# Row maxima subtracted by extra rows of the queries, fetched by DMA, in place of one-hot matmuls

## The reference

```python
# layer 0:  LN; softmax(q k^T * 9**-0.5) over keys; MLP = mixture of 4 experts, top 2
# layer 1:  LN; the same attention; one tanh-GELU MLP
# layer 2:  RMS norm; q and k of each head are RMS-normalised first:
def rmsnorm(x, g, d):
    n = jnp.linalg.norm(x, axis=-1, keepdims=True)
    return x / jnp.maximum(n, EPS) * d ** 0.5 * g        # g is qg for q, kg for k
# layer 3:  LN; attention over the 16 heads of one token, not over tokens
```

## Time and profile before

| | |
|---|---|
| runs, us | 1548.19, 1546.15, 1554.1 (median 1548.19) |
| profiled execution, us | 1548.05 |
| its span, us | 1546.1 |
| mean granted TensorE clock | 0.964 |
| PE busy | 1410.9 us, 91% |
| DVE busy | 1036.5 us, 67% |
| ACT busy | 779.5 us, 50% |
| POOL busy | 541.6 us, 35% |
| attention of layer 0 (first to last exponential) | 64.8 to 242.5 |
| of layer 1 | 585.4 to 756.0 |
| of layer 2 | 892.9 to 1097.8 |
| of layer 3 | 1224.7 to 1448.8 |

### The profile page before, as it was taken

The page is one execution under the profiler, slowest core; times in us unless marked ns, Lnnn a source line. Parts: engine busy times, 40 slices in busy tenths (PEclk is TensorE's granted clock), DMA queues, the critical chain, the costliest instruction groups (busy, mean ns, idle before and its releaser), DMA issues. The chain is left out here.

```text
span 1546.1 us, 41104 instructions
## 1 busy us (share of the span) xinstructions
PE 1410.9 (91%) x16016; PEld 1055.9 (68%) x16016; DVE 1036.5 (67%) x2601; ACT 779.5 (50%) x1287; POOL 541.6 (35%) x739
## 2 busy tenths in 40 slices
PE   5799988999999998999999688877999799998998
PEld 2377676777777776777777566666776577776776
DVE  4698885666776677888447689897355466665342
ACT  2377664333323336676555366665544365555543
POOL 3355542211131304554323324433335134343222
PEclk9799999999999999999999899999999799999999
DMA  4765631111122123554001333453207576774011
GB/s 129 161 151 155 148 95 52 51 44 44 36 70 70 33 73 87 144 146 120 20 29 46 105 94 92 110 129 86 45 24 108 90 109 114 132 131 93 25 54 47
DMA packets 209129, 134.94 MB, mean 87 GB/s; under 512 B 142461, under 2 KB 191320, under 8 KB 202730
## 3 DMA queue, kind: packets, MB, share of 16 engines
q1 hardware_dynamic: 188978, 129.74, 35.3%
q10 hardware_dynamic: 19960, 2.57, 1.2%
HBM read 98.24 MB, written 33.24 MB: 85 GB/s over the span
## 5 line engine op out<-in xcount | busy, mean ns | idle before, releaser
L1546 DVE TENSOR_REDUCE negm<-banks 128x8 bf16<-128x1024 f32 x256 | 311.0, 1215 | 81.4 <-PE banks L650 79.6
L1235 ACT ACTIVATE prob<-banks 128x1024 f32<-128x1024 f32 x256 | 262.5, 1025 | 191.9 <-PE banks L672 191.1
L1363 ACT ACTIVATE hid<-banks 128x512 f32<-128x512 f32 x144 | 86.0, 597 | 220.3 <-PE banks L961 220.2
L1977 POOL TENSOR_TENSOR X<-X,gx 128x288 f32<-128x288 f32 x128 | 104.1, 826 | 255.0 <-DVE gx L1576 253.2
L977 PEld LDWEIGHTS banks<-wfc,hid 128*128 128x128 f32 x1152 | 156.6, 190 | 29.9 <-issue 20.3
L668 PE MATMUL banks<-qk 54*128 54x128 bf16 (+1 forms) x2048 | 168.7, 236 | 5.3 <-ACT prob L1235 5.0
L672 PE MATMUL banks<-mT,identb 64*128 64x128 bf16 x2048 | 165.7, 225 | 0.9 <-issue 0.9
L977 PE MATMUL banks<-wfc,hid 128*128 128x144 f32 x1152 | 161.1, 286 | 0.0
L650 PE MATMUL banks<-qk 54*128 54x128 bf16 (+1 forms) x2048 | 122.9, 241 | 39.6 <-DVE negm L1546 24.9
L960 PE MATMUL banks<-hT,wfc 128*128 128x512 f32 x288 | 149.6, 601 | 2.4 <-DMA wfc<-in_L_cond_w 2.4
L684 PE MATMUL banks<-prob,V 128*32 128x128 f32 x4096 | 143.5, 282 | 0.0
(11 more groups left out here) (169 smaller groups left out, 2777.0 us busy)
## 6 DMA issues: line engine op xcount, KB each, us to landing
qk<-qk_scr SPq DMA_DIRECT2D x96, 216.0 KB
gbuf<-gate_scr SPq DMA_DIRECT2D x64, 288.0 KB, 4.5
qk_scr<-parts SPq DMA_DIRECT2D x48, 288.0 KB, 2.8
qk<-qk_scr SPq DMA_DIRECT2D x96, 144.0 KB
qk<-cw_scr SPq DMA_DIRECT2D x8, 1024.0 KB, 4.9
qk_scr<-parts SPq DMA_DIRECT2D x48, 144.0 KB, 2.4
qk<-qk_scr SPq DMA_DIRECT2D x96, 72.0 KB
qk<-tok_scr SPq DMA_DIRECT2D x32, 216.0 KB
```

The costliest lines, as they stand in the source:

```text
L1235: act.activation(prob[:, 2 * (U % 3):2 * (U % 3) + 2, :], pairs[1][:], ACT.Exp, scale=scale).then_inc(a_exp, 1)
L1546: dve.tensor_reduce(negm[:, u // 2, :, 4 * (u % 2):4 * (u % 2) + 4], pairs[0][:].rearrange("q s (h k) -> q s h k", k=T), AX.X, ALU.max, ne ...
L1977: pool.tensor_tensor(x, x, gx[:, q, :, :], ALU.add).then_inc(g_x, 1)
```

## The change

In layers 0 to 2 an operand of `scores` has 62 rows instead of 54. On the side of the keys the 8 new rows of each half are constants: row j is one for head j and zero for the others; SyncE loads them from `io.picks`, once for each slot, and slot 1 again before group 10, since layer 0's MLP uses that room. On the side of the queries row j holds row j of `mT`, repeated for all 8 heads; ScalarE issues two DMAs for each pair, from `mT` into `qk`, right behind the exponential of an even unit, three units ahead of the one that needs it (`row_of_maxima`); the first two pairs of a layer go ahead of its first exponential. `scores` waits for these DMAs (q_m) instead of for `mT`. The one-hot matmuls stay in layer 3 alone.

In layer 2 `head_norms` is gone from VectorE. GpSimd's `scale_heads` multiplies the factors by the gain (two operations), then q and then k by the factors, all four sequences in one operation each. It stands ahead of `parts23` of the same group, behind `copy_rest` of the group before, and in layer 1's MLP behind `factor`. VectorE does Newton rounds 2 and 3 both at unit 0.

```diff
+RM = KS
-        def operand(l, side, n, U, s, i):
+        def operand(l, side, n, U, s, i, more=0):
-            rows = KS if l < 3 else KS + TB
+            rows = KS + more if l < 3 else KS + TB
...
+            def picking_rows(r):
+                for s in range(2):
+                    row = 64 * s + RM
+                    sp.dma_start(qk[row:row + 8, 1, r].rearrange("j h t -> j (h t)").bitcast(F32), io.picks).then_inc(q_one[r], 16)
...
-                    pe.wait_ge(d_qn, CR + 8 * (n - 16) + (8 if m else 4))
+                    pe.wait_ge(g_qn, CR + 2 * (n - 16) + (2 if m else 1))
...
-                pe.wait_ge(d_mt, CR + U // 2 + 1)
+                if l < 3:
+                    if u == 0 and n in (0, 1, 2, 10):
+                        pe.wait_ge(q_one[n % 3], 64 if n == 10 else 32)
+                    if u % 2 == 0:
+                        pe.wait_ge(q_m[U // 2 % 2], 32 * (U // 4 + 1))
+                else:
+                    pe.wait_ge(d_mt, CR + U // 2 + 1)
                 for i in range(4):
                     at = slice(T * i, T * i + T)
                     for s in range(2):
-                        pe.matmul(bank[2 + s][:, at], operand(l, 1, n, U, s, i), operand(l, 0, n, U, s, i),
-                                  start=True, stop=False)
-                    for s in range(2):
+                        mm = pe.matmul(bank[2 + s][:, at], operand(l, 1, n, U, s, i, 8), operand(l, 0, n, U, s, i, 8),
+                                       start=True, stop=l < 3)
+                    for s in range(2 if l == 3 else 0):
...
+            def row_of_maxima(P):
+                act.wait_ge(d_mt, CR + P + 1)
+                for s in range(2):
+                    row = 64 * s + RM
+                    act.dma_start(qk[row:row + 8, 0, P // G % 3, :, T * (P % G):T * (P % G) + T],
+                                  mT[64 * s:64 * s + 8, P % G, :].unsqueeze(1).to_broadcast([8, 8, T])) \
+                        .then_inc(q_m[P % 2], 16)
...
+                if l < 3:
+                    row_of_maxima(32 * l)
+                    row_of_maxima(32 * l + 1)
                 weights(l, 64 * l)
...
                         if U + 1 < last:
                             weights(l, U + 1)
+                        if l < 3 and u % 2 == 1 and U + 3 < last:
+                            row_of_maxima((U + 3) // 2)
...
-                        if l == 2 and 0 < g < 6 and u <= 1:
-                            head_factors(n + 2, False, (u + 2,))
-                        if l == 2 and g < 6 and 1 <= u <= 2:
-                            head_norms(n + 2, u - 1)
+                        if l == 2 and 0 < g < 6 and u == 0:
+                            head_factors(n + 2, False, (2, 3))
...
-                        for side in range(2):
-                            head_norms(N + (g - 4) // 2, side)
...
+            def scale_heads(n):
+                r = n - 16
+                qs, _ = by_token(n)
+                pool.wait_ge(d_nw, CR + 12 * (r + 1))
+                for side in range(2):
+                    x = rs[:, :, H * side:H * side + H]
+                    pool.tensor_scalar(x, x, gains[:, 2 + side:3 + side], None, ALU.mult).then_inc(g_rg, 1)
+                pool.wait_ge(a_qt, CR + 4 * (r + 1))
+                for side in range(2):
+                    pool.wait_ge(g_rg, CR + 2 * r + side + 1)
+                    v = qs[:, :, C * side:C * side + C].rearrange("t b (d h) -> t b d h", d=D)
+                    pool.tensor_tensor(v, v, rs[:, :, H * side:H * side + H].unsqueeze(2).to_broadcast([T, G, D, H]),
+                                       ALU.mult).then_inc(g_qn, 1)
```

More of the change, by code:

```diff
@@ L243, in build @@
         q_wq = [sem(f"q_wq{i}") for i in range(L - 1)]
+        q_one, q_m = [sem(f"q_one{r}") for r in range(3)], [sem("q_m0"), sem("q_m1")]
         q_gs, q_out = [sem(f"q_gs{l}") for l in range(L)], sem("q_out")
@@ L260, in build @@
         d_on, d_onr, d_gate, d_ss = sem("d_on"), sem("d_onr"), sem("d_gate"), sem("d_ss")
-        d_nw, d_qn, d_top, d_cw, d_y = sem("d_nw"), sem("d_qn"), sem("d_top"), sem("d_cw"), sem("d_y")
+        d_nw, g_qn, g_rg, d_top, d_cw, d_y = sem("d_nw"), sem("g_qn"), sem("g_rg"), sem("d_top"), sem("d_cw"), sem("d_y")
         g_zero, g_set, g_ra, g_rb, g_rc = sem("g_zero"), sem("g_set"), sem("g_ra"), sem("g_rb"), sem("g_rc")
@@ L343, in _ @@
             sp.dma_start(X[:, 3 * G:4 * G, :], xv[:, 3 * G:4 * G, :]).then_inc(q_x[3], 16)
+            picking_rows(0)
+            picking_rows(1)
             def load_first(k, done):
@@ L427, in read_parts @@
                     sp.wait_ge(s_mod, CR + L)
+                    if n == 1:
+                        picking_rows(2)
                 if n >= 3:
@@ L434, in read_parts @@
                     sp.wait_ge(d_hg, CR + NT * (1 if n == 8 else 8))
+                if n == 10:
+                    picking_rows(1)
                 sp.wait_ge(q_w, written(n))
@@ L1424, in _ @@
             for x in (d_set, d_wa, d_ws, d_mod, d_stat, d_mv, d_hm, d_hr, d_r1, d_sm, d_mt, d_rec, d_on, d_onr, d_gate,
-                      d_ss, d_nw, d_qn, d_top, d_cw, d_y, d_rep, d_xn, d_ms, d_hg, d_bi, d_ct, d_gl):
+                      d_ss, d_nw, d_top, d_cw, d_y, d_rep, d_xn, d_ms, d_hg, d_bi, d_ct, d_gl):
                 dve.sem_inc(x, CR)
@@ L1518, in head_factors @@
                     dve.wait_ge(d_nw, done + 2)
-                    dve.wait_ge(d_qn, CR + 8 * r)
+                    dve.wait_ge(g_qn, CR + 2 * r)
                     dve.tensor_scalar(y.bitcast(I32), t.bitcast(I32), -1.0, float(MAGIC), ALU.mult, ALU.add) \
@@ L1528, in head_factors @@
                     dve.scalar_tensor_tensor(y, t, 1.5, y, ALU.add, ALU.mult).then_inc(d_nw, 1)
[L1530 to L1539, removed]
             def head_max(l, U):
@@ L1904, in _ @@
         def _(pool):
-            for x in (g_zero, g_set, g_ra, g_rb, g_rc, g_rd, g_rs, g_xn, g_xr, g_p2, g_p3, g_x, g_ew, g_ox):
+            for x in (g_zero, g_set, g_ra, g_rb, g_rc, g_rd, g_rs, g_xn, g_xr, g_p2, g_p3, g_x, g_ew, g_ox, g_qn, g_rg):
                 pool.sem_inc(x, CR)
@@ L2011, in attention @@
                         pool.wait_ge(g_x, CR + 2 * m0)
+                    if l == 2 and g < 6:
+                        scale_heads(n + 2)
                     if g < 6:
@@ L2029, in mlp @@
                         factor(k)
+                    if l == 1 and g in (4, 6):
+                        scale_heads(N + (g - 4) // 2)
                     if g == 0:
@@ L2090 @@
     io.block_mask = put("block_mask", np.stack([np.where(own, 0.0, MASK), own], axis=1).astype(np.float32))
+    picks = np.repeat(np.eye(8, dtype=np.uint32) * 0x3F803F80, TG // 2, axis=1)
+    io.picks = put("picks", picks.view(np.float32))
     io.gains = [given("L2_cond_" + x) for x in ("g1", "g2", "qg", "kg")]
```

## The result

The changed kernel takes 1664.65 us (median of 4 runs, 1656.41 to 1668.45) where the kernel before, in runs beside it, takes 1551.14 (4 runs, 1546.15 to 1554.69): ratio 1.0727, 95% interval 1.067 to 1.0785, so 7.3% slower. Forecast were 1589 us and a range up to 1640. The direction was right; the loss is 113 us where 41 were forecast.

What follows compares the result with a forecast made beforehand. TensorE and VectorE were taken to bound the attention stages in lockstep, with the transfer behind VectorE in layer 2. 1548 - 13 - 5 + 55 + 4 = 1589 us, range 1527 to 1640.

Steps and rivals of the forecast that it cites:

- (a): One-hot matmuls gone from scores in layers 0 to 2: 13 us saved, of 44 if TensorE were the path everywhere.
- (b): Layer 2's head_norms leaves VectorE: 5 us saved, bounds 0 and 14.4.
- (c): GpSimd's scaling of q and k in layer 2: price 0; 12 us if its operations took twice as long.
- (d): Row of maxima by DMA in layers 0 to 2: copies land late beside reads, 55 us lost, bounds 0 and 115.
- the sequencer runs ahead of the engine: In the copies' step: ScalarE's two issues of some 0.3 us hide under the 1.02 us exponential.
- (e): Layer starts: first scores wait for the first copies, 4 us lost, bounds 0 and 8.
- ScalarE itself is held up: Rival: landings of 8.9 us and issues of 1.1 us that outlast the exponential, 1649 us, chance 0.12.
- The copies land inside the lead: Rival: row copies land in time for the scores, within the 4.2 us lead; 1534 us, chance 0.33.
- The half-way rival: Landings of 5.0 to 5.3 us lose 16 to 22 us, cancelling the savings; 1548 us, chance 0.13.
- its sum with 8.9 us: The copies' loss if they land in 8.9 us, as the engine-sharing rule would have it: 115 us.

Runs made afterwards that it cites:

- e1: The kernel before with GpSimd's scale_heads in place of head_norms; one-hot matmuls kept, no row copies: 1550.11 us, ratio 0.9992.
- e9: e1 with neither one-hot matmuls nor row copies in layers 0 to 2, so the maxima are not subtracted there: 1535.68 us, ratio 0.9935.
- e10: e9 with the changed kernel's 192 row copies issued but used by no scores: 1561.61 us, ratio 1.0127.
- e11: The kernel before, each read of 18 or 27 rows in layers 0 to 2 cut into 16 rows and the rest: 1598.62 us, ratio 1.037.
- e8: The changed kernel, but in layers 0 and 1 SyncE waits for each two of a group's twelve reads: 1684.59 us, ratio 1.0859.
- e15: The changed kernel, reads of groups 3 to 7 of layers 0 and 1 cut to 256 bytes of each row: 1590.88 us, ratio 1.0262.
- e5: The changed kernel with maxima 7 units ahead instead of 5 in layers 0 to 2: 1688.59 us, ratio 1.0903.
- e14: e10 with its 192 unused copies cut to 256 bytes each, issued at the same places: 1554.84 us, ratio 1.0027.

## Why the prediction was wrong

On the scale of 1550 us the change adds up as: scaling -1 (e1), one-hot matmuls -9 (e1 to e9), copies that nobody waits for +30 (e9 to e10), waiting for them +93 (e10 to the changed kernel, with the lower clock and the loads of the constants), together +113.

- **(a) the matmuls, 13 us.** Right: 9 by the ratios, 14 by the medians. Of the 44 us that all the units would give, a fifth to a third is on the path; the waits for On said a third.
- **(b) head_norms, 5 us of 0 to 14.4.** Too much: 1 us, with an interval of -3 to +6 around it. What VectorE gave back went into the wait for the reads, 5.3 to 7.8 us in e1, which the step named and then priced too low.
- **(c) GpSimd, 0.** Right (e1).
- **(d) the copies, 55 us of 0 to 115: the step that failed, in two terms.** The issues were sized at 0.3 us each and hidden under the exponential. They take 0.70, two outlast the exponential by 0.4 us, and OT's copy behind them, which nobody had priced, is what TensorE then waits for. With the traffic, which these runs do not separate from it, the price is 26 to 30 us. The sentence "the sequencer runs ahead of the engine" was true and did not help, since the next activation stands behind the issues in the same sequencer. The waiting was sized by one landing, 6.3 us, of a copy under the first loads. The number of waits came near: 2.1 pairs in each of 18 bursts, 38, were forecast, and 32 found. The size of one was 1.8 us in layers 0 and 1 and 0.6 to 0.8 in layer 2; measured are 3.3 in the mean (105.6 / 32), 3.9 in layer 1, 1.8 in layer 2. The landing was too short. The copies' first pieces wait for those of the reads, as counted above. In layers 0 and 1 the last update of the copies that were waited for beside reads comes at 8.1 us in the median, and they are wanted at 4.8: 3.4 us, where the mean wait is 3.6. The prediction's own sum with 8.1 us in place of 6.3 gives 8.8 - 5.2 = 3.6 for such a pair. The row of a copy beside reads, 8.9 us, served as the bound only. On top the lower clock after a wait lengthens the work behind it.
- **(e) the starts, 4 us.** 17 in the trace: 9.6 at layer 0, where the copies met the first loads. Their last update comes 13.7 us after the issue. The part that was worked out, 2.2 us at layer 1, is 2.7 there.

Of the rivals, "ScalarE itself is held up" (1649 us, 0.12) had both mechanisms and came within 1% of the time; it should have had the larger chance once issues of 1.13 and 1.45 us stood in the rows. "The copies land inside the lead" holds for 56 of the 57 quiet pairs, and for 8 of the 38 beside reads. The half-way rival's sum is 16 to 25 us by its own factors (0.8 x 2.6 x 12), not 16 to 22; this changes no chance.

The rule of the Trainium skill (DMA: Bandwidth & Descriptors, "Why a DMA increments its semaphore by 16 and not by 1") on how many engines share a copy is borne out by the updates of the semaphores. Each read of 9, 18 or 27 rows has nine from the engines, each row copy eight, and in e11 the reads of 16, 11 and 2 rows have sixteen, eleven and two. The share in a burst goes with it, 0.64 and 0.93. The prediction tied its sum with 8.9 us to this and to the order of a semaphore's increments; the last update came at 7.7 us. It came 0.39 us behind the last packet when quiet and 0.86 beside reads, so little of the delay arises there. The same page's "Queues, rings and completion order" says that an engine takes turns between queues a packet of descriptors at a time. The counts above agree with turns, and here one turn of the reads is about eleven pieces of 8 KB to an engine. Fewer reads (e8) or fewer bytes (e15) ahead shorten it.

The remedies tried gave nothing: none of the kernels that leave nothing out beats the kernel before, and e1 equals it. With the rest of the kernel as it is, the most that another way of subtracting the maxima could gain is e9's 9 to 14 us.

## What to carry to other kernels

Price a DMA in a tight loop by three numbers: its issue time against the instruction beside it and against what stands behind it on the same sequencer; its quiet landing; and its landing beside the largest burst, to the semaphore's last update and not to the last packet, of which the part beyond the lead counts in full. Take that landing from a row beside such reads (8.9 us here) and not from another place (6.3). Before buying lead, look at what else the earlier work needs: here two units of lead freed the copies (105.6 to 8.7 us) and exposed the reads (3.9 to 115.7). And when a short wait is added many times to a busy TensorE, count the granted clock too: 0.97 to 0.88 here.

## What the runs showed of the hardware

- A small copy on one queue was held by the 8 KB pieces queued ahead of it on the other, up to about 100 of them, some eleven to an engine: all but 5 of 63 to 85, 95 to 109 of 117 to 152 (the changed kernel, e5, e10).
- Reads spread over more transfer engines, in 20 DMAs instead of 12, were slower: share 0.64 to 0.93, a piece of 8 KB 528 to 805 ns, 153 to 123 GB/s in the burst (e11).
- An issue on ScalarE's queue takes 0.70 us for 64 pieces of 256 bytes, 0.63 for 8, and 0.60 for 16 pieces of 16 bytes; most of it does not depend on the pieces.
- A contiguous copy of 256 bytes went out as 16 pieces of 16 bytes on sixteen engines (e14).
- The last semaphore update of two quiet copies came 2.81 us after the first issue, 0.4 us after their last packet; beside the reads 7.7 and 0.9 us.
